# A two-layer sequence kernel, first chunk of layer 2: step sizes deferred, norm steps split over two engines, B rows copied from SBUF, filler matmuls in TensorE's gaps

## The chip, the cores and the metric

The kernel runs on one core of a Trainium2 chip, in float32 throughout. The metric is the device time of one launch in microseconds: 20159.46, the median of three runs (20150.19 to 20165.52).

## What is computed

The input is 16 images of 192 channels by 56 x 56, seen as 3136 tokens. Two residual layers follow each other, each behind a group norm without parameters:

```
x = x + L0(gn(x))     # RWKV: WKV recurrences forward and backward, gate, layer norm, output product
x = x + L1(gn(x))     # Mamba: below
# L1, for each token t:
x1 = layernorm(tok) ; x = x1 @ W_in_x.T ; z = x1' @ W_in_z.T
# once forward (f) and once backward (b) over the tokens:
xc  = silu(conv4(x) + conv_b)                  # depthwise, 4 taps, 384 channels
dbl = xc @ W_xproj.T                           # 12 columns for dt, 16 for B, 16 for C
dt  = softplus(dbl[:, :12] @ W_dt.T + dt_bias)
h   = h * exp(dt * A) + (dt * xc) * B          # 384 channels x 16 states, a scan over t
y   = sum over states of h * C + xc * D
out = ((y_f + y_b) * silu(z)) @ W_out.T + b_out
```

## The kernel before

A hardware loop runs over the 16 images; each turn is one block for layer 1 and one for layer 2, with all engines meeting in between (`build`, the loop at its end). Layer 2 is named `layer1_*` in the code, one function for each engine: `layer1_tensor`, `layer1_vector`, `layer1_scalar`, `layer1_pool` (GpSimd) and `layer1_sync` (SyncE, which issues all DMAs).

Layer 2 cuts the tokens into 7 chunks of T = 448 and walks them forward and then backward, 14 chunks (index `i`) in all. In a chunk there are EJ = 3 groups of 128 channels (`e` or `k`), and in a group NP = 8 pairs of states (`p`). The unit is a pair, numbered `q` over the whole layer: 24 in a chunk, 336 in all. For a pair, ScalarE makes two decays exp(dt A) in PSUM (`decay`, L1172) and the values at the pair's boundary (L1181, L1188); VectorE or GpSimd multiplies du = dt xc by two rows of B (`product`, L1021 on VectorE for pairs 1, 3, 4 and 6 of a group, L1232 on GpSimd for 0, 2, 5 and 7); VectorE scans (`scan`, L1032); GpSimd multiplies by two rows of C (`output`, L1240); TensorE sums the result over the states into PSUM by identity matmuls (L962).

What a chunk needs before its first pair is called side work. `side_schedule` puts each such step on its engine's list with a due time counted in pairs, and each engine runs, between its own pairs, what has come due (`Steps.due`, `side(g)`). Times below -10 are the entry of the layer, before any pair. The names of the steps: `ns` scales the input by the group norm (L1060), `n1` sums over channels (L893), `nc` subtracts the mean (L989, L991), `nq` squares (L1067), `n2` sums (L899), `nr` makes the inverse root (L1072, L1074), `nm` multiplies (L1215), `x` is the projection (L905), `xe` its way out of PSUM (L1086), `cv` the convolution by diagonal matrices (L919), `c1` to `c4` and `xc` the silu (L1094 to L1107, L996), `xp` the product for dt, B and C (L926), `p1` its copy to `res` in SBUF (L1114), `t` the product for the step size (L931), `t1` to `t3` and `td` the softplus (L1121 to L1130, L1001), `du` the product dt xc (L1221), `dp` its copy to PSUM for VectorE (L1134). `res` holds the 12 dt rows in partitions 0 to 11, B's 16 rows in partitions 32 to 47 and C's in 48 to 63.

A B or C row is needed in all 128 partitions. SyncE stores the 32 rows to DRAM (`cw`, L1286, 56 KB) and loads them back with every row repeated to 128 partitions, four rows at a time: `bl` (L1292) for B and `cl` (L1297) for C, k = 0 to 3, alternating, 896 KB each. Pair p needs `bl` number p // 2.

PSUM has eight banks: 0 to 3 hold the decays of two pairs, 4 holds du, 5 the sum y, 6 and 7 serve the side work. At the entry of the layer banks 0 to 3 serve side work as well, and the first decays wait until the side jobs in them are done. The entry does the whole chain for chunk 0 with all three groups' step sizes, in this order on the lists:

```
for e in range(EJ):
    step_size(i, e, t + u[e])
```

## Time and profile before

| | |
|---|---|
| median of 3 runs | 20159.46 us |
| profiled execution, its time | 20123.45 us |
| its span, first to last instruction | 20121.7 us |
| mean granted TensorE clock | 0.938 |
| TensorE matmuls, busy | 17468.9 us, 87% |
| VectorE, busy | 17219.6 us, 86% |
| GpSimd, busy | 16825.7 us, 84% |
| ScalarE, busy | 13992.6 us, 70% |
| DMA, mean share of 16 engines | 29.8% |

The profiled execution is one run of the same program. Times inside it count from the start of its span; the first image's layer 2 begins at 228.51. An L and a number is a line of the kernel before. A float32 matmul of the program appears as two instructions, each with its weight load.

### The profile page before, as it was taken

What the parts mean: (1) busy time and instruction counts of PE and PEld (TensorE: products, weight loads), DVE (VectorE), ACT (ScalarE), POOL (GpSimd) and SP (SyncE); (2) the same over time, 40 slices, a digit from 0 to 9 for tenths busy, and PEclk for the clock granted to TensorE, in tenths of its full rate; (3) what the DMA queues carried; (4) which work ended last, traced back from release to release, by engine and by line L of the source; (5) the groups of instructions that cost most, each with busy time, mean ns of one, the idle gap of its engine ahead of it and who ended that gap; (6) DMA issues with size and microseconds to landing.
All of it is one profiled execution on the core that took longest, in us unless ns stands there. A gap on an engine that the chain in (4) does not pass through costs nothing. (4 is left out here: it accounts for less than half of the span.)

```text
span 20121.7 us, 179901 instructions
## 1 busy us (share of the span) xinstructions
PE 17468.9 (87%) x43392; PEld 7664.0 (38%) x43392; DVE 17219.6 (86%) x13583; ACT 13992.6 (70%) x35077; POOL 16825.7 (84%) x10932
## 2 busy tenths in 40 slices
PE   7888988889888898888988889888898888988889
PEld 3433434334343343433434334343343433434334
DVE  7988979889798897988979789797897978979789
ACT  6767767577676776767767577675776767767677
POOL 6978969789697896978969799696996979969699
PEclk9989989899899998989989899898998989989899
DMA  2313323133231332313323133231332313323233
GB/s 85 135 65 129 137 76 134 65 129 137 76 134 66 128 137 76 134 65 128 137 77 133 66 128 136 77 133 65 129 136 76 134 65 135 130 77 135 73 132 124
DMA packets 528855, 2178.88 MB, mean 108 GB/s; under 512 B 96328, under 2 KB 243424, under 8 KB 527648
## 3 DMA queue, kind: packets, MB, share of 16 engines
q1 hardware_dynamic: 527648, 2165.99, 29.8%
q8 instruction: 366, 6.00, 0.1%
q14 instruction: 841, 6.89, 0.1%
HBM read 1905.47 MB, written 245.63 MB: 107 GB/s over the span
## 5 line engine op out<-in xcount | busy, mean ns | idle before, releaser
L1032 DVE TENSOR_TENSOR_SCAN arena<-ps,arena 128x897 f32<-128x897 f32 x5376 | 10963.7, 2066 | 993.9 <-ACT arena L1188 761.6
L1240 POOL TENSOR_TENSOR arena<-arena 128x896 f32<-128x896 f32 x5376 | 9427.4, 1769 | 901.5 <-PE ps L962 619.8
L962 PE MATMUL ps<-arena,ident 128*128 128x448 f32 x21504 | 8979.4, 556 | 879.6 <-POOL arena L1240 876.2
L1172 ACT ACTIVATE ps<-arena,A 128x448 f32<-128x448 f32 x10752 | 6412.1, 632 | 1749.0 <-DVE arena L1032 1705.3
L962 PEld LDWEIGHTS ps<-arena,ident 128*128 128x128 f32 x21504 | 4049.3, 193 | 5473.3 <-issue 3690.3
L1232 POOL TENSOR_TENSOR arena<-arena 128x896 f32<-128x896 f32 x2688 | 4773.6, 1776 | 0.2 <-DMA arena<-bc_rows 0.2
L1021 DVE TENSOR_TENSOR arena<-ps,arena 128x896 f32<-128x896 f32 x2688 | 2868.0, 1067 | 30.4 <-ACT ps L1134 30.4
L919 PE MATMUL ps<-arena,diag 128*128 128x448 f32 x5376 | 2178.4, 549 | 154.0 <-issue 141.8
L919 PEld LDWEIGHTS ps<-arena,diag 128*128 128x128 f32 x5376 | 1014.8, 192 | 1233.9 <-issue 1097.4
L1094 ACT ACTIVATE arena<-ps,vece 128x448 f32<-128x448 f32 x672 | 423.3, 630 | 948.5 <-PE ps L919 948.5
L1188 ACT ACTIVATE arena<-arena 128x2 f32<-128x2 f32 x5376 | 1045.8, 195 | 50.9 <-DVE arena L1032 50.9
L956 PE MATMUL ps<-arena,skipd 128*128 128x448 f32 x1344 | 720.3, 619 | 389.6 <-DVE arena L1008 268.0
L1221 POOL TENSOR_TENSOR arena<-arena 128x448 f32<-128x448 f32 x672 | 653.3, 980 | 461.7 <-DVE arena L1001 461.7
L774 POOL TENSOR_TENSOR arena<-arena 128x448 f32<-128x448 f32 x336 | 343.6, 1023 | 735.0 <-DVE arena L547 735.0
L1181 ACT ACTIVATE arena<-arena 128x1 f32<-128x1 f32 x4608 | 888.4, 193 | 0.0
L996 DVE TENSOR_TENSOR arena<-arena,ps 128x448 f32<-128x448 f32 x672 | 407.8, 607 | 436.7 <-ACT ps L1107 435.9
L593 PE MATMUL ps<-x,arena 96*128 96x448 f32 x1344 | 688.6, 651 | 77.1 <-DVE arena L563 46.9
L1215 POOL TENSOR_TENSOR arena<-arena 96x448 f32<-96x448 f32 x224 | 214.7, 979 | 628.6 <-ACT arena L1074 628.6
L905 PE MATMUL ps<-arena,wx 96*128 96x448 f32 x1344 | 601.7, 590 | 136.0 <-POOL arena L1215 136.0
L931 PE MATMUL ps<-arena,wdt 12*128 12x448 f32 x1344 | 665.3, 592 | 47.5 <-DVE arena L1001 37.4
L785 POOL TENSOR_TENSOR arena<-arena 128x448 f32<-128x448 f32 x336 | 359.9, 1071 | 404.2 <-ACT arena L731 404.2
L576 DVE TENSOR_TENSOR_SCAN ps<-ps,arena 128x898 f32<-128x898 f32 x336 | 680.4, 2025 | 3.1
(160 smaller groups left out, 19406.9 us busy)
## 6 DMA issues: line engine op xcount, KB each, us to landing
arena<-bc_rows SPq DMA_DIRECT2D x1792, 896.0 KB, 5.4
x_projected<-arena SPq DMA_DIRECT2D x112, 672.0 KB, 3.5
y_forward<-arena SPq DMA_DIRECT2D x112, 672.0 KB, 3.9
arena<-x_projected SPq DMA_DIRECT2D x112, 672.0 KB, 7.7
arena<-y_forward SPq DMA_DIRECT2D x112, 672.0 KB, 4.1
x<-in_x SPq DMA_DIRECT2D x119, 336.0 KB, 3.6
x_normed<-arena SPq DMA_DIRECT2D x112, 336.0 KB, 2.8
arena<-x_normed SPq DMA_DIRECT2D x112, 336.0 KB, 4.2
```

Source lines behind the costliest of these rows:

```text
L576: e.tensor_tensor_scan(atile(u), atile(u), bq[:, u % 3, :], 0.0, ALU.mult, ALU.add).then_inc(b_sc, 1)
L593: k = e.matmul(ps[:, b, 0:T], ws[:, i, o:o + 128], f[:, i, :], **last)
L919: m = e.matmul(o, diag[:, k, q, :], xh[i % 2][:, k, h:h + T], start=q == 0, stop=q == 3)
L956: e.matmul(y, skipd[:, s, k, :], xc[:, r % NXC, :], start=True, stop=False)
L962: m = e.matmul(y, ident[:, :], pr[:, q % NPR, a * T:a * T + T], start=False, stop=p == NP - 1 and a == 1)
L1021: e.tensor_tensor(two(bb[:, q % NB, :]), ps[:, DUBANK, 0:T].unsqueeze(1).to_broadcast([128, 2, T]), br[:, 2 * p:2 * p + 2, :], ALU.mult).t ...
L1032: e.tensor_tensor_scan(rev(hh[:, q % NH, 0:W2], s), rev(decays(q)[:, 0:W2], s), rev(bb[:, q % NB, 0:W2], s), car[:, k, n:n + 1] if i % NC ...
L1172: e.activation(two(decays(q))[:, a, :], dt[:, r % NDT, :], ACT.Exp, scale=Am[s][:, k, 2 * p + a:2 * p + a + 1]).then_inc(c_ex, 1)
L1181: e.activation(bb[:, q % NB, T:T1], car[:, k, n:n + 1] if i % NC else zero[:, 0, 0:1], ACT.Copy).then_inc(c_rs, 1)
L1188: e.activation(car[:, k, 2 * p:2 * p + 2], h[:, 0:T1 + 1:T1] if s else h[:, T - 1:W2:T1], ACT.Copy).then_inc(c_ca, 1)
L1232: e.tensor_tensor(two(bb[:, q % NB, :]), du[:, r % NDU, :].unsqueeze(1).to_broadcast([128, 2, T]), br[:, 2 * p:2 * p + 2, :], ALU.mult).th ...
L1240: e.tensor_tensor(pr[:, q % NPR, :].rearrange("p (a b) -> p a b", a=2), two(hh[:, q % NH, :]), cr[:, 2 * p:2 * p + 2, :], ALU.mult).then_i ...
```

## The change

Four things change, all at the entry of layer 2 in every image.

1. *Step sizes.* Of chunk 0, group 0's step size stays in the entry; those of groups 1 and 2 get the due times -1.9 and 1, so `t`, `t1` to `t3`, `td` and `du` of these run between the first pairs. Banks 0 to 3 serve only jobs below -10.
2. *Norm steps of chunk 0 on two engines.* `ns`, `nq` and `nm` do the first half (96 x 448) on ScalarE, ScalarE and GpSimd as before and the second half on VectorE.
3. *B's first four rows.* In chunk 0, SyncE copies rows 0 and 1 from `res` in SBUF to 128 partitions each (one DMA for a row, source one partition repeated 128 times, semaphore `s_bf`), then stores the 32 rows as before, then copies rows 2 and 3 in the same way; `bl` number 0 is left out. Pair 0 waits for `s_bf`, pair 1 for both copies of `s_bl[0]`.
4. *Fillers.* `busy(e, n, b)` issues n matmuls of constants, 128 x 384, into a bank that nobody reads then: five at the end of layer 1, two behind the statistics, two behind `n1`, three behind `n2`, three behind the last `cv`, one behind `xp`.

```diff
@@ -79,11 +79,12 @@
         act.append((max(NP * (EJ * i + e) - 2, t + 4.5), "dp", i, e))
 
     def project(i, t, u, v):
+
         pe.append((t, "xp", i, 0))
         act.append((t + v, "p1", i, 0))
         sp.append((t + 1.5, "cw", i, 0))
         for e in range(EJ):
-            step_size(i, e, t + u[e])
+            step_size(i, e, t + u[e] if i or not e else (-1.9, 1)[e - 1])
         for G in range(4):
             r = PER * i - NP + 2 * G
             sp.append((max(r + 1, t + 2), "bl", i, G))
@@ -103,6 +104,8 @@
             pe += [(t - 0.2, "n1", i, 0), (t + 2.1, "n2", i, 0)]
             act += [(t + 1.9, "nq", i, 0), (t + 3.0, "nr", i, 0), (t + 4.6, "xh", i, 0)]
             pool += [(t + 3.4, "nm", i, 0)]
+            if not i:
+                dve += [(t + 1.9, "nq", i, 0), (t + 3.4, "nm", i, 0)]
             sp += [(t + 5, "nw", i, 0), (t + 8, "xw", i, 0)]
             for e, (u, v) in enumerate(((4.2, 6.4), (4.3, 7.4), (6.2, 11))):
                 pe.append((t + u, "x", i, e))
@@ -136,11 +139,11 @@
     plans = [sorted(p, key=lambda a: a[0]) for p in (pe, act, dve, pool, sp)]
     jobs, used = {}, {}
     for k, (t, name, i, e) in enumerate(plans[0]):
-        banks = WBANK if t >= 0 else [*WBANK, 0, 1, 2, 3]
+        banks = WBANK if t >= -10 else [*WBANK, 0, 1, 2, 3]
         b = banks[k % len(banks)]
         jobs[name, i, e] = (k, b, used.get(b, 0))
         used[b] = used.get(b, 0) + 1
-        if t < 0:
+        if t < -10:
             first = dict(used)
     return plans, jobs, first
@@ -578,6 +581,11 @@
         w.wait_ge(b_ag, 2 + 2 * NC)
         for j in range(CJ):
             e.bn_aggr(mv[:, j, :], st[:, j, :, :].rearrange("p a b -> p (a b)"))
+
+    def busy(e, n, b):
+
+        for _ in range(n):
+            e.matmul(ps[:, b, 0:3 * 128], ident[:, :], skipd[:, 0, :, :].rearrange("p a b -> p (a b)"), start=True, stop=True)
 
     def layer0_tensor(e):
         w = Waits(e)
@@ -678,6 +686,8 @@
                 w.wait_ge(b_bv, U)
                 product(VB, 1, *divmod(U, 3)).then_inc(b_v, 1)
             side(U)
+        w.wait_ge(b_xo, nth(4, 1) + 1)
+        busy(e, 5, 3)
 
     def layer0_scalar(e):
         e.preload_act_table_set("natural_log_exp_and_others")
@@ -833,9 +843,10 @@
                                                             "taps_loaded", "x_stored"))
     s_xl, s_nl, s_yl = ([sem(f"{k}{b}") for b in range(2)] for k in ("xp_loaded", "n_loaded", "y_loaded"))
     s_bl, s_cl = ([sem(f"{k}{G}") for G in range(4)] for k in ("b_loaded", "c_loaded"))
+    s_bf = sem("b_first")
     sems1 = [n1.v, n1.t, n1.a, c_ex, c_rs, c_bv, c_bp, c_sc, c_ca, c_mc, c_sm, c_ya, c_yv, c_wt, *c_wf, c_ns, c_nc,
              c_nq, c_nr, c_nm, c_pad, c_xh, c_c1, c_c2, c_c3, c_c4, c_t1, c_t2, c_t3, c_du,
-             c_dp, c_z1, c_z2, c_z3, c_z4, c_g, s_nw, s_xw, s_yw, s_cw, s_dg, s_out, *s_xl, *s_nl, *s_yl, *s_bl, *s_cl]
+             c_dp, c_z1, c_z2, c_z3, c_z4, c_g, s_nw, s_xw, s_yw, s_cw, s_dg, s_out, *s_xl, *s_nl, *s_yl, *s_bl, *s_cl, s_bf]
 
     def filled(w, name, i, e=0):
         w.wait_ge(c_wt, jobs[name, i, e][0] + 1)
@@ -861,6 +872,13 @@
         b = DECAY[q % 2]
         return ps[:, b:b + 2, :].rearrange("p a b -> p (a b)")[:, 0:2 * T1]
 
+    def b_loaded(w, i, p):
+
+        if not i and not p:
+            w.wait_ge(s_bf, 32)
+        else:
+            w.wait_ge(s_bl[p // 2], 16 * (i + 1 + (p < 2)))
+
     def product_done(w, q):
 
         if ON_VECTOR[q // NP % EJ][q % NP]:
@@ -876,7 +894,11 @@
     def layer1_tensor(e):
         w = Waits(e)
         n1.tensor(e, w, 0)
+        busy(e, 2, DUBANK)
         steps = Steps(plan_pe)
+
+
+        behind = {("n1", 0): 2, ("n2", 0): 3, ("cv", 2): 3, ("xp", 0): 1}
 
         def job(name, i, k):
             _, b, n = jobs[name, i, k]
@@ -943,6 +965,8 @@
                         m = e.matmul(o[0:CP, :], wout[:, j, k * CP:(k + 1) * CP], gy[:, j, :],
                                      start=j == 0, stop=j == EJ - 1)
                     m.then_inc(c_wt, 1)
+                if not i:
+                    busy(e, behind.get((name, k), 0), DUBANK)
 
         side(-10)
         for g in range(-2, Q + LAG):
@@ -968,6 +992,8 @@
     def layer1_vector(e):
         w = Waits(e)
         w.wait_ge(n1.v, n1.vector(e, w, 0))
+        e.tensor_scalar(nrm[:, 0, T:2 * T], x1[:, 1, ch(0)], gs[:, 4, 1:2], gs[:, 5, 1:2], ALU.mult,
+                        ALU.add).then_inc(c_ns, 1)
         e.memset(xh[0][:, :, 0:3], 0.0).then_inc(c_pad, 1)
         for b in DECAY:
             e.memset(ps[:, b, T:T1], 0.0)
@@ -989,6 +1015,14 @@
                     e.tensor_tensor(o, o, ps[0:CP, b, 0:T], ALU.subtract).then_inc(c_nc, 1)
                     o = nrm[:, i % 2, T:2 * T]
                     e.tensor_tensor(o, o, ps[0:CP, b, 0:T], ALU.subtract).then_inc(c_wf[b], 1)
+                if name == "nq":
+                    freed(w, "n1", i)
+                    o = nrm[:, i % 2, T:2 * T]
+                    e.tensor_tensor(tmp[:, 1, :], o, o, ALU.mult).then_inc(c_nq, 1)
+                if name == "nm":
+                    w.wait_ge(c_nr, i + 1)
+                    o = nrm[:, i % 2, T:2 * T]
+                    e.tensor_tensor(o, o, tmp[:, 2, :], ALU.mult).then_inc(c_nm, 1)
                 if name == "xc":
                     w.wait_ge(c_c4, r + 1)
                     b = bank_of("cv", i, k)
@@ -1016,7 +1050,7 @@
         def product(q):
             r, i, k, p, s = pair(q)
             w.wait_ge(c_dp, r + 1)
-            w.wait_ge(s_bl[p // 2], 16 * (i + 1))
+            b_loaded(w, i, p)
             w.wait_ge(c_sc, q - NB + 1)
             e.tensor_tensor(two(bb[:, q % NB, :]), ps[:, DUBANK, 0:T].unsqueeze(1).to_broadcast([128, 2, T]),
                             br[:, 2 * p:2 * p + 2, :], ALU.mult).then_inc(c_bv, 1)
@@ -1056,14 +1090,14 @@
                     if i > 1:
                         filled(w, "x", i - 2, EJ - 1)
                         w.wait_ge(s_nw, 16 * (i - 1))
-                    for j in range(CJ):
+                    for j in range(CJ if i else 1):
                         e.activation(nrm[:, i % 2, j * T:j * T + T], x1[:, j, ch(c)], ACT.Identity,
                                      scale=gs[:, 4, j:j + 1], bias=gs[:, 5, j:j + 1]).then_inc(c_ns, 1)
                 if name == "nq":
                     freed(w, "n1", i)
                     w.wait_ge(c_nc, i + 1)
                     w.wait_ge(c_nm, 2 * i)
-                    for j in range(CJ):
+                    for j in range(CJ if i else 1):
                         e.activation(tmp[:, j, :], nrm[:, i % 2, j * T:j * T + T], ACT.Square).then_inc(c_nq, 1)
                 if name == "nr":
                     filled(w, "n2", i)
@@ -1210,7 +1244,7 @@
                 if name == "nm":
                     w.wait_ge(c_nr, i + 1)
                     freed(w, "n1", i)
-                    for j in range(CJ):
+                    for j in range(CJ if i else 1):
                         o = nrm[:, i % 2, j * T:j * T + T]
                         e.tensor_tensor(o, o, tmp[:, 2, :], ALU.mult).then_inc(c_nm, 1)
                 if name == "du":
@@ -1227,7 +1261,7 @@
         def product(q):
             r, i, k, p, s = pair(q)
             w.wait_ge(c_du, r + 1)
-            w.wait_ge(s_bl[p // 2], 16 * (i + 1))
+            b_loaded(w, i, p)
             w.wait_ge(c_sc, q - NB + 1)
             e.tensor_tensor(two(bb[:, q % NB, :]), du[:, r % NDU, :].unsqueeze(1).to_broadcast([128, 2, T]),
                             br[:, 2 * p:2 * p + 2, :], ALU.mult).then_inc(c_bp, 1)
@@ -1281,10 +1315,14 @@
             if name == "cw":
                 freed(w, "xp", i)
                 for G in range(4 if i >= 2 else 0):
-                    w.wait_ge(s_bl[G], 16 * (i - 1))
+                    w.wait_ge(s_bl[G], 16 * (i - (G > 0)))
                     w.wait_ge(s_cl[G], 16 * (i - 1))
+                for n in range(0 if i else 2):
+                    e.dma_start(br[:, n, :], res[32 + n:33 + n, :].unsqueeze(1).to_broadcast([1, 128, T])).then_inc(s_bf, 16)
                 e.dma_start(cd[i % 2], res[32:64, :]).then_inc(s_cw, 16)
-            if name == "bl":
+                for n in range(2, 2 if i else 4):
+                    e.dma_start(br[:, n, :], res[32 + n:33 + n, :].unsqueeze(1).to_broadcast([1, 128, T])).then_inc(s_bl[0], 16)
+            if name == "bl" and (i or k):
                 w.wait_ge(s_cw, 16 * (i + 1))
                 if i:
                     for q in (PER * i - NP + 2 * k, PER * i - NP + 2 * k + 1):
```

On SyncE, at chunk 0's store and loads (`bc_rows` is the DRAM tensor, `arena` is SBUF, `c_free0` the semaphore of `p1`), before:

```order
L1286 DMA bc_rows<-arena 32x448 [waits c_free0]
L1292 DMA arena<-bc_rows 128x1792 [waits bc_stored]
L1297 DMA arena<-bc_rows 128x1792
L1292 DMA arena<-bc_rows 128x1792
L1297 DMA arena<-bc_rows 128x1792
```

and with the change:

```order
L1321 DMA arena<-arena 128x1x448 [waits c_free0]
L1321 DMA arena<-arena 128x1x448
L1322 DMA bc_rows<-arena 32x448
L1324 DMA arena<-arena 128x1x448 x2
L1335 DMA arena<-bc_rows 128x1792 [waits bc_stored]
L1330 DMA arena<-bc_rows 128x1792
L1335 DMA arena<-bc_rows 128x1792
```

Four copies from `arena` to `arena` stand around the store, and the first load is now C's, where B's stood.

On GpSimd, from the norm's multiply on (96x448; then du, 128x448; B products, 128x2x448; output products, 128x896), before:

```order
L1215 TENSOR_TENSOR arena<-arena 96x448 [waits c_free6,c_nrs]
L1215 TENSOR_TENSOR arena<-arena 96x448
L1221 TENSOR_TENSOR arena<-arena 128x448 [waits c_free3,c_free1]
L1221 TENSOR_TENSOR arena<-arena 128x448 [waits c_free6,c_free2]
L1221 TENSOR_TENSOR arena<-arena 128x448 [waits c_free7,c_free3]
L1232 TENSOR_TENSOR arena<-arena 128x2x448 [waits b_loaded0,c_du]
L1232 TENSOR_TENSOR arena<-arena 128x2x448 [waits b_loaded1]
L1240 TENSOR_TENSOR arena<-arena 128x896 [waits c_loaded0,c_scan]
L1240 TENSOR_TENSOR arena<-arena 128x896 [waits c_scan]
L1240 TENSOR_TENSOR arena<-arena 128x896 [waits c_loaded1,c_scan]
L1232 TENSOR_TENSOR arena<-arena 128x2x448 [waits b_loaded2]
```

and with the change:

```order
L1249 TENSOR_TENSOR arena<-arena 96x448 [waits c_free6,c_nrs]
L1255 TENSOR_TENSOR arena<-arena 128x448 [waits c_free3,c_free1]
L1266 TENSOR_TENSOR arena<-arena 128x2x448 [waits b_first,c_du]
L1266 TENSOR_TENSOR arena<-arena 128x2x448 [waits b_loaded1]
L1274 TENSOR_TENSOR arena<-arena 128x896 [waits c_loaded0,c_scan]
L1274 TENSOR_TENSOR arena<-arena 128x896 [waits c_scan]
L1255 TENSOR_TENSOR arena<-arena 128x448 [waits c_free6]
L1274 TENSOR_TENSOR arena<-arena 128x896 [waits c_loaded1,c_scan]
L1266 TENSOR_TENSOR arena<-arena 128x2x448 [waits b_loaded2]
L1249 TENSOR_TENSOR arena<-arena 96x448 [waits c_free7,c_nrs]
L1249 TENSOR_TENSOR arena<-arena 96x448
```

The second and third du moved behind output products 2 and 4, and one half of the first multiply is gone; the second B product still stands ahead of the first output product.

On TensorE, from the statistics to the convolution, before:

```order
L333 MATMUL ps<-mv,grp 96x2
L335 MATMUL ps<-gs,grp 96x2 [waits c_stat_vec]
L893 MATMUL ps<-arena,ones 96x448 [waits c_nsc]
L893 MATMUL ps<-arena,ones 96x448
L899 MATMUL ps<-arena,ones 96x448 [waits c_nsq]
L899 MATMUL ps<-arena,ones 96x448
L905 MATMUL ps<-arena,wx 128x448 [waits c_nrm]
L905 MATMUL ps<-arena,wx 128x448 x5
L919 MATMUL ps<-arena,diag 128x448 [waits c_pad,c_free0]
```

and with the change:

```order
L336 MATMUL ps<-mv,grp 96x2
L338 MATMUL ps<-gs,grp 96x2 [waits c_stat_vec]
L588 MATMUL ps<-skipd,ident 128x384 x2
L915 MATMUL ps<-arena,ones 96x448 [waits c_nsc]
L915 MATMUL ps<-arena,ones 96x448
L588 MATMUL ps<-skipd,ident 128x384 x2
L921 MATMUL ps<-arena,ones 96x448 [waits c_nsq]
L921 MATMUL ps<-arena,ones 96x448
L588 MATMUL ps<-skipd,ident 128x384 x3
L927 MATMUL ps<-arena,wx 128x448 [waits c_nrm]
L927 MATMUL ps<-arena,wx 128x448 x5
L941 MATMUL ps<-arena,diag 128x448 [waits c_pad,c_free0]
```

L588 is the filler; the waits of the rows that were there are the same.

## Rows read from the trace of the kernel before

**Rows 1.** The page: busy us, share of the span and instructions of each engine.

```profile
PE 17468.9 (87%) x43392; PEld 7664.0 (38%) x43392; DVE 17219.6 (86%) x13583; ACT 13992.6 (70%) x35077; POOL 16825.7 (84%) x10932
```

**Rows 2.** Timeline of image 1: start us, us, engine, line, operation [idle before <-releaser].

```profile
223.66 1.00 PE L657 MATMUL ps<-arena,wo 64*96 64x448 f32 x4
...
230.99 1.41 ACT L1060 ACTIVATE arena<-x,gs 96x448 f32<-96x448 f32 x2 [0.22 <-DVE gs L328]
...
232.46 3.30 PE L893 MATMUL ps<-arena,ones 96*96 96x448 f32 x4 [2.35 <-ACT arena L1060]
...
236.98 1.04 ACT L1067 ACTIVATE arena<-arena 96x448 f32<-96x448 f32 x2 [4.57 <-DVE arena L991]
...
238.07 3.30 PE L899 MATMUL ps<-arena,ones 96*96 96x448 f32 x4 [2.31 <-ACT arena L1067]
...
242.73 1.91 POOL L1215 TENSOR_TENSOR arena<-arena 96x448 f32<-96x448 f32 x2 [38.97 <-ACT arena L1074]
```

**Rows 3.** The same timeline, from the projection x to p1.

```profile
244.69 7.66 PE L905 MATMUL ps<-arena,wx 96*128 96x448 f32 x12 [3.32 <-POOL arena L1215]
...
252.19 9.19 PE L919 MATMUL ps<-arena,diag 128*128 128x448 f32 x24
...
266.27 0.54 ACT L1114 ACTIVATE arena<-ps 64x448 f32<-64x448 f32 x1 [1.71 <-PE ps L926]
```

**Rows 4.** The same timeline, from the first step size on.

```profile
268.06 0.64 ACT L1121 ACTIVATE arena<-ps,vece 128x448 f32<-128x448 f32 x1 [1.25 <-PE ps L931]
...
275.33 0.98 POOL L1221 TENSOR_TENSOR arena<-arena 128x448 f32<-128x448 f32 x1 [0.69 <-DVE arena L1001]
...
276.26 3.50 POOL L1232 TENSOR_TENSOR arena<-arena 128x896 f32<-128x896 f32 x2
...
278.16 3.93 DVE L1032 TENSOR_TENSOR_SCAN arena<-ps,arena 128x897 f32<-128x897 f32 x2
...
280.25 1.76 POOL L1240 TENSOR_TENSOR arena<-arena 128x896 f32<-128x896 f32 x1 [0.49 <-DVE arena L1032]
...
285.38 1.67 PE L899 MATMUL ps<-arena,ones 96*96 96x448 f32 x4
```

**Rows 5.** GpSimd's groups, 280 to 349 us: busy, mean ns, idle before.

```profile
L1240 POOL TENSOR_TENSOR arena<-arena 128x896 f32<-128x896 f32 x24 | 42.1, 1766 | 6.4 <-DVE arena L1032 4.9 <-PE ps L962 1.5
```

**Rows 6.** Windows: us, five engines busy, PEclk granted, DMA share, GB/s.

```profile
222.00:226.00 4.00, 2.66 (x10) 0.81 (x8) 3.86 (x8) 0.00 (x0) 0.00 (x0) 1.00 0.00 0
...
232.50:235.70 3.20, 3.20 (x4) 0.91 (x4) 0.00 (x0) 0.00 (x0) 0.00 (x0) 0.50 0.00 0
```

**Rows 7.** VectorE's groups, 194 to 230 us.

```profile
L516 DVE TENSOR_TENSOR arena<-arena 128x448 f32<-128x448 f32 x2 | 1.4, 698 | 0.0
```

**Rows 8.** DMA issues (KB, us to landing); then the first and third load alone.

```profile
arena<-arena SPq DMA_DIRECT2D x128, 112.0 KB, 2.2
bc_rows<-arena SPq DMA_DIRECT2D x224, 56.0 KB, 1.6
```

```profile
L1292 SPq DMA_DIRECT2D arena<-bc_rows x1: 343/343/343, 268.4 to 268.4; - x1
...
DMA to landing us min/median/max: 4.5/4.5/4.5
```

```profile
L1292 SPq DMA_DIRECT2D arena<-bc_rows x1: 432/432/432, 269.3 to 269.3; - x1
...
DMA to landing us min/median/max: 8.3/8.3/8.3
```

**Rows 9.** Windows while DMAs read 128, 64 and 32 partitions of SBUF.

```profile
255.00:255.50 0.50, 0.50 (x2) 0.21 (x2) 0.00 (x0) 0.10 (x1) 0.00 (x0) 1.00 1.02 383
87.10:87.60 0.50, 0.00 (x0) 0.00 (x0) 0.50 (x2) 0.50 (x2) 0.50 (x1) 1.00 0.89 204
267.65:267.85 0.20, 0.20 (x2) 0.03 (x1) 0.00 (x0) 0.00 (x0) 0.00 (x0) 0.50 0.99 224
```

## The prediction

> **What bounds the kernel now.** I read the page's busy shares first [rows 1]. No engine is idle much: TensorE 87%, VectorE 86%, GpSimd 84%. The change touches only the stretch in which each image enters layer 2, so the page's averages say little about it. I therefore read the timeline from the end of layer 1 (image 1, 223 to 282 us), then the landing times of the DMAs there, then windows with the granted clock and the DMA rate. One image stands for all 16: each of them shows this stretch once.
>
> The entry is a chain in which one engine works at a time. From 230.99 on, ScalarE scales both halves of the input, TensorE sums, VectorE subtracts, ScalarE squares, TensorE sums again, ScalarE takes the inverse root, GpSimd multiplies [rows 2]. Then come the projection x, the convolutions, the product xp and the copy p1, which ends at 266.81 [rows 3]. I call that moment P. After P, three groups' step sizes are computed before GpSimd's first B product at 276.26 and the first scan at 278.16, P+11.35 [rows 4]. From there on GpSimd is nearly full: over the first chunk its output products alone take 42.1 us and wait 6.4 us [rows 5].
>
> TensorE runs much of this entry at the lower of its two levels, 1.2 of 2.4 GHz: the granted clock is 1.00 from 222 to 226 and 0.50 from 232.5 to 235.7 [rows 6]. The same four instructions of 448 columns take 3.30 us there [rows 2] and 1.67 us in chunk 1's norm at 285.38 [rows 4]. In between the engine had no dense work from 224.66 to 232.46.
>
> **Up to P, part by part.**
> - *Fillers.* Nothing reads them. The five at layer 1's end start at 224.66, behind the last L657 [rows 2]. Each is two instructions of 384 columns; at 1.67/4 = 0.42 per 448 columns at most, ten cost 3.6 us and end by 228.3, inside the wait for the next block at 228.51. Those behind n1 (1.4 us) fit the 2.3 us before n2, those behind n2 (2.1 us) the 3.3 before x, those behind the last convolution (2.1 us) the 3.9 between the last convolution's end (261.38) and the last third of xp, of which the first two thirds need 1.5. The one behind xp costs t at most 0.1. Hence zero, if the clock stays up; at half clock they double, and the cover over n1 and n2 is overrun by about 2 us together.
> - *What the clock gives.* n1 and n2 go from 3.30 to 1.67: 2 x 1.63. The 12 instructions of x start at 244.69 and hand over at 252.19 [rows 3]; at the upper level 12 x 0.375 = 4.5, so 3.0 less. The 24 of the convolutions take 9.19, 0.38 each, and gain nothing. Sum 6.3. The bounds are 6.3 and, with the fillers useless, minus 2. I take 6.3, since the work up to 226 ran at 1.00 and the fillers leave no gap near today's eight microseconds.
> - *Norm steps on two engines.* The scaling takes 1.41 on ScalarE alone; halved, 0.70 less. The squares take 1.04; VectorE's nearest row, L516, takes 0.70 [rows 7], so 0.3 less. The multiply takes 1.91 on GpSimd; GpSimd's half is 0.98, so 0.9 less if both run together. Sum 1.9; the bounds are 1.2 (the multiply's halves in turn, 0.98 + 0.70) and 1.9. I take 1.9: two products of GpSimd take 3.50 from 276.26 although VectorE's first scan starts beside them [rows 4].
> - The Trainium skill (SBUF — State Buffer, "Who interferes with whom") says a VectorE instruction with two SBUF inputs and a GpSimd instruction that reads SBUF exclude each other. By that rule the multiply would gain 0.2 instead of 0.9, 11 us over 16 images; no row of this entry shows the pair.
>
> P comes 6.3 + 1.9 = 8.2 us earlier.
>
> **After P.** The later groups' step sizes leave the path. What remains: t's product (1.2 us from P to L1121), four passes of ScalarE of 0.54 to 0.64 (2.3), at most 0.70 on VectorE, 0.98 for du, 1.75 for the product [rows 3, 4]: with the hand-overs scan 0 could start at about P+7.3, 4 us earlier, **if B is there**. The two du move in behind scans 0 and 1: 2 x 0.98 on GpSimd, which is the full engine; the td go to VectorE, the t1 to t3 to ScalarE.
>
> **B's first rows decide.** Now: the store lands 1.6 us after its issue, and the first load (bl0), issued at 268.43, lands 4.5 later, at P+6.1. The third (bl1) lands at 277.6, P+10.8, just before GpSimd's second product at about P+11.2 [rows 8]. So loads land 2.3 us apart.
>
> The change sends each of four rows 128 times out of one partition: 128 x 1792 B = 229 KB per row, 0.92 MB in all, as much as the load it replaces. No row shows a DMA with one source partition. The nearest ones [rows 9]: a store out of 128 partitions, 383 GB/s at a share of 1.02; a copy from 64 partitions to 64, 204 GB/s at 0.89; the store out of 32 partitions, 224 GB/s at 0.99. A busy DMA engine thus moves 23.5 GB/s in the first case and 14.2 in the other two: with fewer partitions two engines share a path of about 28 GB/s, they don't each keep theirs. If all 16 queue at the one path of partition 32 (33, 34, 35), a row takes 229/28 = 8.1 us. Ends of the range: 0.6 us per row (no shared path, 383 GB/s) and 9.8 us (one engine's 23.5). I take 8.1, which is what the nearest rows say of a path.
>
> The Trainium skill (SBUF — State Buffer, "Door 1: The DMA port swizzle") puts partitions 32 to 35 on one port and gives 27.6 GB/s measured over four partitions; that would be 8.3 us a row and 0.8 us more per image than my sum. It speaks against this part of the change.
>
> Then rows 0 and 1 land at about P + 1.6 + 16.2 = P+17.9 (1.6 is the small copy's 2.2 without its 0.6 of transfer). The store's packets stand behind them and rows 2 and 3 behind those; all four are through by P+34. The load cl0, issued when the store lands, has its packets behind rows 2 and 3 and lands at P+36.2, bl1 at P+38.4 (2.3 each). On GpSimd the second product (pair 2, needs bl1) stands ahead of the first output product. So it starts at P+38.4, the output product at P+40.2 instead of P+13.4: 26.8 later. Add 2.0 for the two du, subtract 4 of the 6.4 us that GpSimd idled in this chunk: 24.8. Against 8.2 earlier: 16.6 us later per image, 266 us in 16. The profiled execution's 20123 becomes 20389; the median of the runs lies 36 above it, so **20425 us**. With 7 to 9.8 us a row, and with the clock's share uncertain, this case spans 20320 to 20545.
>
> **Rivals.**
> - *The rows leave at full rate (28%).* Each row takes 0.6 us, rows 0 and 1 land by P+3.5, and the store by P+3.2 to 3.7. Then bl1 becomes what the first chunk waits for: issued at about P+3.7, it lands at P+10.0, GpSimd's second product ends at P+11.8 and the output product starts 1.6 earlier than now. The du fit into the 6.4 us of idle. 8.2 + 1.8 = 10 us per image, 160 in all: 20000. For it: the load out of DRAM repeats its source 128 times too, at full rate (0.92 MB per 2.3 us). Against it: the lower rate per engine in [rows 9].
> - *A path twice as wide (9%).* At 4 us a row all four are through by P+17, bl1 lands at P+21.6, the output product starts 10 later; with du and idle 8 remains against 8.2: within 0.2% of now, 20160.
> - *The fillers don't hold the clock.* Then 8.2 shrinks to about 0 (minus 2 of the fillers, plus 1.9); it shifts either case by up to +130 us. It decides nothing about the sign in the first case, and is in the ranges.
> - *The loads don't matter because the step sizes bound the start.* Scan 0 waits today for td and du, not for B; but B has only 3 us of slack there (276.26 against 272.9), and 16 us of transfer don't fit in.
>
> **Numbers.** Shared path 63%, full rate 28%, wider path 9%. A measurement of this kernel tells 0.2% (40 us) from no change. Faster: 0.29 (the full rate, a little of the middle). Same: 0.08. Slower: 0.63. The range must reach into both cases: 19980 to 20540; the likeliest case's own is 20320 to 20545.
>
> **What would show it.** Right: the four single-row copies out of SBUF land 16 us and more after issue; GpSimd's and VectorE's first products wait for DMAs; the DMA rate in that stretch is near 28 GB/s; the first output product starts some 40 us after p1; PEclk is 1.00 from the block's start to P, n1 and n2 at 1.67, P at 30 us after the block's start instead of 38.3. Wrong: landings of 2 to 4 us for these copies, a first scan near P+7.3, and GpSimd's second product waiting for bl1 at P+10.

## The result, and the profile after

The changed kernel takes **20450.1 us** (median of 4 runs, 20445.8 to 20463.2); the kernel before took 20154.8 us beside it (4 runs, 20132.9 to 20165.5). The ratio of the two sets of runs is **1.0151, 95% interval 1.0136 to 1.0166**: 1.5% slower. (The quotient of the two medians is 1.0147; ratios below, too, can differ from the quotient of the medians by some 0.0005.) The forecast was 20425 us, in the case of the shared path. The profiled execution took 20451.14 us (span 20449.3), so here it lies at the median; the profiled execution of before, 20123.45, lay 36 below the median of its first three runs.

The timeline of image 1 after the change, in the stretch that the prediction is about (start us, us, engine, line, operation [idle before <-releaser]). The block of layer 2 opens with ScalarE's table load at 231.47.

```profile
227.55 3.49 PE L588 MATMUL ps<-skipd,ident 128*128 128x384 f32 x10
...
231.47 1.28 ACT L1079 ACT_TABLE_LOAD   x1 [14.40 <-PEq L1356]
...
234.47 1.74 PE L915 MATMUL ps<-arena,ones 96*96 96x448 f32 x4 [0.30 <-ACT arena L1094]
...
241.17 0.62 DVE L1025 TENSOR_TENSOR arena<-arena 96x448 f32<-96x448 f32 x1 [3.11 <-ACT arena L1108]
241.21 1.41 POOL L1249 TENSOR_TENSOR arena<-arena 96x448 f32<-96x448 f32 x1 [34.49 <-ACT arena L1108]
...
242.68 4.78 PE L927 MATMUL ps<-arena,wx 96*128 96x448 f32 x12 [0.89 <-POOL arena L1249]
...
261.38 0.54 ACT L1148 ACTIVATE arena<-ps 64x448 f32<-64x448 f32 x1 [1.71 <-PE ps L948]
```

These are the rows that answer to [rows 2, 3]. The four instructions of n1 take 1.74 instead of 3.30, x takes 4.78 instead of 7.66, and p1 ends at 261.92: P, the end of the copy p1, is 30.45 behind the table load, where it was 38.3 in image 1 of before. The ten instructions of the five fillers at layer 1's end are done at 231.04, 0.43 before the table load.

Behind P, the same timeline:

```profile
261.94 1.18 SPq L1321 DMA_DIRECT2D arena<-arena  x2
...
263.15 5.64 SPq L1322 DMA_DIRECT2D bc_rows<-arena  x1
...
268.84 10.55 SPq L1324 DMA_DIRECT2D arena<-arena  x2
...
281.44 1.77 POOL L1266 TENSOR_TENSOR arena<-arena 128x896 f32<-128x896 f32 x1 [14.31 <-DMA arena<-arena]
282.42 4.62 SPq L1335 DMA_DIRECT2D arena<-bc_rows  x1
287.08 8.54 SPq L1330 DMA_DIRECT2D arena<-bc_rows  x1
...
298.16 1.09 DVE L1055 TENSOR_TENSOR arena<-ps,arena 128x896 f32<-128x896 f32 x1 [32.09 <-DMA arena<-arena]
...
303.03 1.77 POOL L1266 TENSOR_TENSOR arena<-arena 128x896 f32<-128x896 f32 x1 [19.82 <-DMA arena<-bc_rows]
304.76 3.48 POOL L1274 TENSOR_TENSOR arena<-arena 128x896 f32<-128x896 f32 x2
```

They answer to [rows 4]. GpSimd's first B product waits 14.31 us for a copy, VectorE's 32.09 us, and GpSimd's next one 19.82 us for the load bl1. The first output product starts at 304.76, P+42.8, where it was P+13.4. On the page the waits are these:

```profile
L1266 POOL TENSOR_TENSOR arena<-arena 128x896 f32<-128x896 f32 x2688 | 4768.3, 1774 | 543.9 <-DMA arena<-bc_rows 315.3
L1055 DVE TENSOR_TENSOR arena<-ps,arena 128x896 f32<-128x896 f32 x2688 | 2862.1, 1065 | 513.5 <-DMA arena<-arena 513.5
```

Before, the same two groups had waited 0.2 and 30.4 us. The copies' landing times, rows 0 and 1 and then rows 2 and 3 (views of the lines L1321 and L1324; the three durations in ns are those of the issue on SyncE, the landing times count from the start of the issue):

```profile
L1321 SPq DMA_DIRECT2D arena<-arena x32: 524/563/596, 261.9 to 19398.0; - x32
...
DMA to landing us min/median/max: 10.7/14.8/18.8
```

```profile
L1324 SPq DMA_DIRECT2D arena<-arena x32: 1958/5256/8547, 268.8 to 19412.9; - x32
...
DMA to landing us min/median/max: 20.6/21.4/22.1
```

And windows of the same kernel (us, five engines, granted clock, DMA share, GB/s): the statistics, n1 of chunk 0, n1 of chunk 1, and the copies:

```profile
231.50:234.00 2.50, 1.86 (x8) 1.07 (x8) 1.12 (x6) 2.01 (x4) 0.00 (x0) 1.00 0.03 7
234.50:236.20 1.70, 1.70 (x5) 0.88 (x6) 0.00 (x0) 0.00 (x0) 0.00 (x0) 1.00 0.00 0
269.30:272.50 3.20, 3.20 (x4) 0.90 (x4) 0.00 (x0) 3.10 (x7) 0.00 (x0) 0.50 0.90 27
264.00:280.00 16.00, 3.30 (x4) 0.96 (x4) 0.62 (x1) 7.64 (x16) 0.98 (x1) 0.61 0.89 27
```

The granted clock of TensorE, which was 0.50 in the norm (1.2 of 2.4 GHz) [rows 6], is 1.00 through chunk 0's norm now. During the copies the 16 DMA engines are busy nine tenths of the time and move 27 GB/s together; in [rows 9] shares of 0.89 to 1.02 went with 204 to 383. In this kernel a high DMA share alone says little of how much moves.

One image is no mean, so for this kernel and all that follow I read four marks from the trace in each of the 16 images: the table load that opens the block, P, the starts of the first scan and the first output product (counted from P), and the start of the 25th scan, the first of chunk 1. The last column is the ratio of the times to before, with its interval, where there is one. Each kernel is compared with runs of before taken beside it: e1 to e4 with 15 runs (median 20140.2), e5 to e8 with 15 (20115.3), e9 to e12 with 9 (20130.6).

| kernel | block to P | first scan | first output | 25th scan | ratio |
|---|---|---|---|---|---|
| before | 38.60 | 11.13 | 13.23 | 81.16 | 1 |
| the change | 30.44 | 37.26 | 42.70 | 111.13 | 1.0151 (1.0136 to 1.0166) |
| e1: without the SBUF rows | 30.44 | 7.95 | 12.47 | 81.12 | 0.9922 (0.9909 to 0.9936) |
| e2: the SBUF rows alone | 38.68 | 37.26 | 42.75 | 109.94 | 1.0217 (1.0201 to 1.0232) |
| e3: fillers alone | 32.00 | 10.90 | 13.00 | 80.92 | 0.9919 (0.9905 to 0.9932) |
| e4: deferred step sizes alone | 38.59 | 7.91 | 12.43 | 81.14 | 0.9997 (0.9988 to 1.0006) |
| e5: norm split alone | 36.00 | 12.03 | 14.13 | 82.16 | 1.0002 (0.9993 to 1.0011) |
| e6: e1, bl1 ahead of cl0 | 30.44 | 7.96 | 10.83 | 81.16 | 0.9929 (0.9915 to 0.9942) |
| e7: e1, fillers after P too | 30.44 | 7.98 | 12.49 | 79.77 | 0.9915 (0.9901 to 0.9928) |
| e8: rows from partitions 32 to 47 | 30.44 | 12.72 | 18.91 | 87.10 | one run |
| e9: rows from 16 of partitions 0 to 60 | 30.44 | 7.88 | 13.88 | 81.24 | one run |
| e10: two SBUF rows | 30.44 | 24.44 | 29.92 | 97.94 | 1.0052 (1.0037 to 1.0067) |
| e11: e7 and e6 together | 30.44 | 7.97 | 10.88 | 79.70 | 0.9915 (0.9901 to 0.9928) |
| e12: e3 less the five at layer 1's end | 33.02 | 10.89 | 12.99 | 80.91 | 0.9953 (0.9939 to 0.9966) |

### The profile page after: what moved, and what is told of

Same layout as the page of the kernel before. It is cut to its first block and busy times, and to the rows that moved or that the text cites. A ratio compares the mean times of both kernels' runs of the same rounds, so it can differ in the third digit from the quotient of the medians.

```text
span 20449.3 us, 181005 instructions
## 1 busy us (share of the span) xinstructions
PE 17559.7 (86%) x43904; PEld 7728.2 (38%) x43904; DVE 17248.8 (84%) x13631; ACT 13972.7 (68%) x35045; POOL 16791.7 (82%) x10916
## 5 line engine op out<-in xcount | busy, mean ns | idle before, releaser
L1128 ACT ACTIVATE arena<-ps,vece 128x448 f32<-128x448 f32 x672 | 423.2, 630 | 954.5 <-PE ps L941 954.5
L1215 ACT ACTIVATE arena<-arena 128x1 f32<-128x1 f32 x4608 | 886.4, 192 | 0.0
L1155 ACT ACTIVATE arena<-ps,vece 128x448 f32<-128x448 f32 x672 | 422.7, 629 | 362.8 <-PE ps L953 362.8
L700 ACT ACTIVATE arena<-ps 128x448 f32<-128x448 f32 x336 | 182.1, 542 | 670.6 <-PE ps L606 226.6
```

The costliest lines, as they stand in the source:

```text
L1215: e.activation(bb[:, q % NB, T:T1], car[:, k, n:n + 1] if i % NC else zero[:, 0, 0:1], ACT.Copy).then_inc(c_rs, 1)
```

## The experiments

### e1: all of the change but the SBUF rows

```diff
-        if not i and not p:
-            w.wait_ge(s_bf, 32)
-        else:
-            w.wait_ge(s_bl[p // 2], 16 * (i + 1 + (p < 2)))
+        w.wait_ge(s_bl[p // 2], 16 * (i + 1))
...
-                for n in range(0 if i else 2):
-                    e.dma_start(br[:, n, :], res[32 + n:33 + n, :].unsqueeze(1).to_broadcast([1, 128, T])).then_inc(s_bf, 16)
...
-            if name == "bl" and (i or k):
+            if name == "bl":
```

> The change without its third part: B's first four rows come from DRAM again, all else stays. Theory (the one-partition copies cost all of the loss): the first scan no longer waits for copies; P (end of p1) stays about 30.5 us after the block's start, the first output product starts about 1.6 us earlier after P than before (13.4), so about 10 us per image less than the kernel before: ratio to before near 0.992 (0.990 to 0.995). Rival (the deferred step sizes on the full GpSimd, or the fillers, cost as well): ratio 0.996 to 1.002.

19974.9 us (5 runs, 19959.5 to 19989.4) against 20140.2 (15 runs), 165 us less. Without the copies the rest of the change gains 0.8%, and the first scan starts at P+7.95; the prediction had P+7.3 "if B is there". So the loss is the copies' alone, as expected. The first output product comes 0.8 us earlier than before, not the 1.6 expected, since it waits for the load bl1 (see e6).

### e2: the SBUF rows alone, on the kernel before

The diff is the change's part 3 on before: `b_loaded`, the four copies and the left-out load.

> The third part alone on the kernel before. Theory: the first output product starts about 43 us after P as in the changed kernel, against 13.4 before, so 28 to 30 us per image more: ratio 1.022 to 1.024. Rival (the copies are slow only because the deferral and the idle hand-over put other work beside them): ratio under 1.015.

20570.3 us (4 runs, 20565.4 to 20579.5), 430 us more than before, 26.9 per image, a ratio just under the 1.022 to 1.024 expected. The marks behind P are those of the changed kernel within 0.1 us up to the first output; the 25th scan is 1.2 us earlier. In this kernel no du stand behind the scans, which would account for it. With both parts taken apart, 0.9922 and 1.0217 make 1.0137, near the 1.0151 measured.

### e3: the fillers alone, on the kernel before

```diff
+        w.wait_ge(b_xo, nth(4, 1) + 1)
+        busy(e, 5, 3)
...
+        busy(e, 2, DUBANK)
+        behind = {("n1", 0): 2, ("n2", 0): 3, ("cv", 2): 3, ("xp", 0): 1}
```

Besides these lines it has the helper `busy` and its call behind each job of chunk 0, as in the change.

> The fillers alone on the kernel before. Theory: the granted clock is 1.00 from the block's start to P, n1, n2 and x run at 1.67 to 1.75 and 4.5 us, P comes about 6 us earlier, and as nothing behind P depends on it: 6 us per image, ratio 0.995. But B's loads move with P too, so nothing is lost there. Rival (ScalarE and the loads bound the entry): ratio 0.998 to 1.000.

19978.5 us (5 runs, 19959.2 to 19980.9), 162 us less: as much as e1 gained with three parts, and more than the 0.995 expected. P comes 6.60 us earlier (6.3 had been forecast for the clock), n1, n2 and x take 1.74, 1.75 and 4.78 us as in the changed kernel. 6.6 in 16 images is 106 us; some 56 us more lie elsewhere in the image (see e12).

### e4: the deferred step sizes alone

```diff
-            step_size(i, e, t + u[e])
+            step_size(i, e, t + u[e] if i or not e else (-1.9, 1)[e - 1])
```

With it goes the change's new limit of -10 for banks 0 to 3.

> The deferred step sizes alone on the kernel before. Theory: the first scan comes 3 to 4 us earlier after P, but the second product waits for the third load (P+10.8), and GpSimd has two du more in the chunk: 1 to 2 us per image gained, ratio 0.998 to 0.999. Rival (the du on the full GpSimd cost more than the earlier start brings): ratio 1.000 to 1.002.

20132.7 us (11 runs), ratio 0.9997: nothing that can be measured, where 1 to 2 us per image had been expected. Yet the first scan starts 3.2 us earlier. GpSimd's timeline of image 1 shows where the 3.2 us go:

```profile
283.78 3.48 POOL L1240 TENSOR_TENSOR arena<-arena 128x896 f32<-128x896 f32 x2
287.22 0.98 POOL L1221 TENSOR_TENSOR arena<-arena 128x448 f32<-128x448 f32 x1
288.16 1.76 POOL L1240 TENSOR_TENSOR arena<-arena 128x896 f32<-128x896 f32 x1
289.88 1.77 POOL L1232 TENSOR_TENSOR arena<-arena 128x896 f32<-128x896 f32 x1
294.98 1.91 POOL L1215 TENSOR_TENSOR arena<-arena 96x448 f32<-96x448 f32 x2 [3.32 <-ACT arena L1074]
296.85 1.76 POOL L1240 TENSOR_TENSOR arena<-arena 128x896 f32<-128x896 f32 x1
```

Chunk 1's norm multiply (L1215) stands in GpSimd's order behind three output products and waits 3.32 us for ScalarE's inverse root (2.3 in the mean of the images). In the kernel before it waits for nothing (289.60, behind L1232). The head start runs into chunk 1's norm chain; the fourth output starts at P+24.4 in both kernels in the mean of the images (the last row above is a late one, P+25.6), and from the 12th scan on the two agree within 0.1 us.

### e5: the norm split alone

```diff
+        e.tensor_scalar(nrm[:, 0, T:2 * T], x1[:, 1, ch(0)], gs[:, 4, 1:2], gs[:, 5, 1:2], ALU.mult,
+                        ALU.add).then_inc(c_ns, 1)
...
-                    for j in range(CJ):
+                    for j in range(CJ if i else 1):
```

The squares `nq` and the multiply `nm` are split in the same way; it is the whole of the change's part 2.

> The norm steps on two engines, alone on the kernel before. By the prediction's terms 1.9 us per image less up to P (1.2 if the halves of the multiply exclude each other): ratio 0.9985 to 0.999. Rival (the window in which the granted clock comes back does not move with the work, so the projection only runs longer at the lower level): P - 0 to 0.5 us, ratio 1.000.

20116.7 us (11 runs) against 20115.3 (15 runs): no difference. In the trace P comes 2.6 us earlier, more than the 1.9 of the norm steps, since the projection x also takes less (6.94 for 7.66 in image 1). 0.9 of it is lost again before the first scan. The first four instructions of t now take 0.84 us each, at a granted clock of 0.50 from their start; the kernel before needed 1.91 for its first three, at 0.82 over the first 1.1 us:

```profile
268.51 3.35 PE L933 MATMUL ps<-arena,wdt 12*128 12x448 f32 x4 [0.63 <-ACT arena L1126]
```

At the 25th scan 1.6 us remain, 26 us in all. The interval reaches down to 14 us gained; the one profiled execution (20071.4) is also the lowest of the 11. What became of the rest isn't settled. Alone, the fillers and the split give 6.60 and 2.60 up to P, together 8.16, so they share 1.0 us; x's 0.7 is the larger part of it.

### e6: e1 with the load bl1 ahead of cl0

```diff
-            sp.append((max(r + 3, t + 2.1), "cl", i, G))
+            sp.append((max(r + (3 if i else 3.5), t + 2.1), "cl", i, G))
```

> e1 (B from DRAM) with the second B load ahead of the first C load, in the first chunk. It lands about 8.5 us after P instead of 10.8. Theory A (the wait for this load takes back what the deferral gives): the first output product 1.8 us earlier and the 25th scan too, ratio to before 0.9905 to 0.991. Theory B (the chunk is held at P+22.7 by GpSimd's multiply for chunk 1's norm, whose chain runs on TensorE at the lower clock): the first output products come earlier, the 25th scan doesn't; ratio 0.992 as e1.

19969.9 us (5 runs), ratio 0.9929, as e1. In e1 GpSimd's second B product waits for bl1:

```profile
273.17 1.77 POOL L1263 TENSOR_TENSOR arena<-arena 128x896 f32<-128x896 f32 x1 [2.89 <-DMA arena<-bc_rows]
```

Here the first output comes 1.6 us earlier, and the fourth one at P+24.5 as in e1. Rival 1 of the prediction named this load as the next bound. It is next in order, but chunk 1's norm multiply starts at P+22.6 here as in e1, e4 and before (means of the images), so what the load gives isn't seen.

### e7: e1 with fillers behind the first t and chunk 1's norm sums

```diff
-        behind = {("n1", 0): 2, ("n2", 0): 3, ("cv", 2): 3, ("xp", 0): 1}
+        behind = {("n1", 0, 0): (2, DUBANK), ("n2", 0, 0): (3, DUBANK), ("cv", 0, 2): (3, DUBANK),
+                  ("xp", 0, 0): (1, DUBANK), ("t", 0, 1): (7, YBANK), ("n1", 1, 0): (5, YBANK)}
```

> e1 with fillers also in the two TensorE gaps behind P: seven behind the second group's step product, five behind chunk 1's n1, in the bank of y. Theory B (the first chunk is held by chunk 1's norm chain at the lower clock): n1, the last step product, the skip product and the first sums take half, GpSimd's multiply for chunk 1 starts 2 to 4 us earlier than P+22.7, and the 25th scan with it: ratio 0.989 to 0.991. Theory A (the load bl1 holds it): 0.992 as e1. If the later convolutions of chunk 1 pin it anyway, 0.992 too, with the multiply earlier.

The chain that seems to hold e4 and e6 runs at the lower level: in the changed kernel chunk 1's first norm sums are 3.30 us at a granted clock of 0.50 (window 269.30:272.50 above). With fillers around it, the timeline of e7 reads:

```profile
274.70 1.74 PE L913 MATMUL ps<-arena,ones 96*96 96x448 f32 x4 [0.66 <-ACT arena L1091]
...
276.29 3.39 PE L588 MATMUL ps<-skipd,ident 128*128 128x384 f32 x10
...
280.77 1.01 PE L951 MATMUL ps<-arena,wdt 12*128 12x448 f32 x2 [1.09 <-DVE arena L1032]
```

The norm multiply of chunk 1 on GpSimd waits for ScalarE's inverse root, in image 1 of e1 and then of e7:

```profile
285.01 1.92 POOL L1246 TENSOR_TENSOR arena<-arena 96x448 f32<-96x448 f32 x2 [2.24 <-ACT arena L1105]
```

```profile
288.16 1.92 POOL L1246 TENSOR_TENSOR arena<-arena 96x448 f32<-96x448 f32 x2 [0.44 <-ACT arena L1105]
```

In the mean of the images it moves from P+22.55 to P+21.20, the fourth output from P+24.4 to P+23.1 and the 25th scan by 1.35 us: the head start is held by this chain, shown by shortening it. The gain is less than the 2 to 4 us expected. The fillers quickened more than the norm's own sums. The products that stand ahead of the second sums in TensorE's order, the last of t, the skip product and the first sums over the states, went from 1.86, 1.86 and 2.84 us (image 1 of e1) to 1.01, 1.02 and 1.67 (image 1 of e7). Which of them counts wasn't separated. The time is 19949.7 us (5 runs, 19927.4 to 19958.1). 1.35 in 16 images is 22 us, less than the intervals tell, so that e7 beats e1 rests on the trace alone. It beats both kernels clear of the noise.

### e8: the copies read sixteen neighbouring partitions

```diff
-                    e.dma_start(br[:, n, :], res[32 + n:33 + n, :].unsqueeze(1).to_broadcast([1, 128, T])).then_inc(s_bf, 16)
+                    e.dma_start(br[:, n, :], res[32:48, :].unsqueeze(1).to_broadcast([16, 8, T])).then_inc(s_bf, 16)
```

The same for rows 2 and 3.

> The changed kernel with each of the four one-row copies reading 16 neighbouring partitions (32 to 47) eight times each instead of one partition 128 times; same bytes, same number of packets; B's first four rows are then mixed rows. Theory (four neighbouring partitions share a path of 28 GB/s): 229 KB over 4 paths, 2.0 us a row, the four copies through by about P+10, the first output product near P+21, time 20100 to 20200. Rival (each partition has a path of its own): 0.6 us a row as from 128 partitions, landings of 2.2 to 3.5 us, time near 19990. Rival (the source does not matter, it is the number of small packets): 8 us a row as before, time near 20450.

One run, 20056.3 us, a little under the 20100 to 20200 expected. Bytes and packets are those of the changed kernel, only the sources differ; so the number of small packets isn't what made the copies slow. The views of the first copies and of a window beside them:

```profile
L1321 SPq DMA_DIRECT2D arena<-arena x32: 592/598/627, 263.6 to 19030.4; - x32
...
DMA to landing us min/median/max: 4.4/5.3/6.3
```

```profile
268.00:270.00 2.00, 0.00 (x0) 0.00 (x0) 0.00 (x0) 2.00 (x5) 0.76 (x1) 0.50 0.92 106
```

106 GB/s is four times the 27 of one partition, not sixteen times. So four sources share what one has; with e9, where sources four apart get more, these are four neighbours.

### e9: the copies read sixteen spread partitions

```diff
-                    e.dma_start(br[:, n, :], res[32 + n:33 + n, :].unsqueeze(1).to_broadcast([1, 128, T])).then_inc(s_bf, 16)
+                    e.dma_start(br[:, n, :], res[0:64:4, :].unsqueeze(1).to_broadcast([16, 8, T])).then_inc(s_bf, 16)
```

The same for rows 2 and 3.

> The changed kernel, but each of the four one-row copies reads sixteen partitions spread over the whole of 0 to 60, every fourth one, instead of one partition for all 128 (so the B and C rows are mixed and the output is not the reference's; the bytes and the number of packets are the same). The run before this one read the neighbouring partitions 32 to 47 and moved 104 GB/s, four times the 27 GB/s of one partition. Theory A (only groups of four neighbours share a path): sixteen sources lie in sixteen groups, the sixteen DMA engines run at the full rate of some 200 to 380 GB/s, and the first copies land 2 to 4 us after issue. Theory B (a path is also shared by partitions 32 apart): eight paths of 26 GB/s, 208 GB/s, first copies in 3 to 4 us, all four within 5. Theory C (the source does not matter beyond four paths): landings as in the run before, 4.4 to 6.5 us. Time by A 19980 to 20020 us, by B 20000 to 20040, by C 20056.

```profile
L1321 SPq DMA_DIRECT2D arena<-arena x32: 564/582/594, 258.5 to 18940.3; - x32
...
DMA to landing us min/median/max: 3.0/3.3/3.6
```

```profile
260.00:262.00 2.00, 0.40 (x2) 0.00 (x0) 0.03 (x1) 1.88 (x4) 0.00 (x0) 1.00 1.01 198
```

198 GB/s at a full DMA share: Theory C falls. Sixteen groups of four would allow 16 x 27; the rate is that of eight, as Theory B had it (partitions 32 apart share), and as the copy from 64 partitions had shown (204, [rows 9]). A limit of some 200 GB/s on any copy inside SBUF would give the same rate, though; no run has such a copy with sources above partition 63, so that rival stays open. The time, 19963.9 us, is below what either theory gave and equal to e1's: even when the rows leave SBUF fast, part 3 gains nothing, because the first scan is at P+7.88 against 7.95 from DRAM, and behind it stands chunk 1's chain.

### e10: two rows by copies, two by a load

```diff
-                for n in range(2, 2 if i else 4):
-                    e.dma_start(br[:, n, :], res[32 + n:33 + n, :].unsqueeze(1).to_broadcast([1, 128, T])).then_inc(s_bl[0], 16)
...
+                a = 0 if i or k else 2
+                e.dma_start(br[:, 4 * k + a:4 * k + 4, :],
+                            cd[i % 2, 4 * k + a:4 * k + 4, :].unsqueeze(0).to_broadcast([128, 4 - a, T])).then_inc(s_bl[k], 16)
```

The semaphore waits are set to match.

> The changed kernel with two one-row copies instead of four: rows 2 and 3 of the first groups' B come from the scratch tensor in DRAM after the store, as all B rows did before. Theory A (one path of 27 GB/s, shared by whatever reads those partitions, and everything issued behind it waits): rows 0 and 1 still land at P+19.5, but the store is through by then, the loads behind it are no longer backed up, the first output product comes at about P+26 instead of P+42.8, so 13 to 14 us per image over the version without any copy: 20185 to 20200 us, a ratio of 1.002 to 1.005 to the kernel before; SyncE's issues behind the store return to under 1 us each, those ahead of it may stay long. Theory B (the loss is a fixed delay of the queue whatever is copied): the ratio stays at 1.012 or more. Theory C (two rows are hidden beside the chain of chunk 1's norm): under 0.998.

20238.8 us (4 runs, 20225.4 to 20250.3). Theory A holds in kind: half the rows, somewhat over half the loss (0.0130 of 0.0229 above e1's ratio), and SyncE's issues behind the store take 0.35 to 0.54 us again in the mean of the images. The time lies 39 us above the 20200 at which its range ended. Its P+26 was 3.9 us short: the store lands at P+19.1, only then the load goes out, and VectorE's product that waits for it starts 4.2 us later.

```profile
286.32 1.77 POOL L1266 TENSOR_TENSOR arena<-arena 128x896 f32<-128x896 f32 x1 [13.84 <-DMA arena<-arena]
286.38 0.34 SPq L1329 DMA_DIRECT2D arena<-bc_rows  x1
...
290.56 1.09 DVE L1055 TENSOR_TENSOR arena<-ps,arena 128x896 f32<-128x896 f32 x1 [19.13 <-DMA arena<-bc_rows]
```

The first output is at P+29.92, and the 25th scan 16.8 us later than in e1. The table now shows a pattern for this kernel: in e8, e10 and the change the 25th scan stands 68.0 to 68.4 us behind the first output. Up to P+13 or 14 a delay of the first output costs nothing (e6, e1 and e9: 10.83, 12.47 and 13.88, with the 25th scan at 81.2 each time); beyond that each us costs one.

### e11: the load's order, with the chain shortened

It is e7 with e6's line.

> The fastest version so far (the changed kernel without the on-chip copies, with fillers behind the first group's t and chunk 1's norm products) with the load bl1 issued ahead of cl0. The order alone brought the first output product 1.6 us earlier and nothing in the time when chunk 1's norm chain was cold. Theory A (the chunk is still held by chunk 1's norm and TensorE's products behind it): the ratio to the kernel before is that of the version with the old order, 0.9905 to 0.9920, and the eighth group's output does not move by over 0.3 us. Theory B (with the chain shortened the load is what is late): another 1 us per image, 19930 us, ratio 0.9905 or less.

19966.8 us (5 runs), 0.9915 like e7; the fourth output moves from P+23.1 to P+23.0. Theory A: the load still doesn't bound.

### e12: the fillers without the five at layer 1's end

```diff
-        w.wait_ge(b_xo, nth(4, 1) + 1)
-        busy(e, 5, 3)
```

> The kernel before with the fillers alone, less those at layer 1's end. With all fillers the block of layer 2 took 6.6 us less to P and the time was 0.9919 of the kernel before. Theory A (each filler holds the clock only for the products next to it): without those five the block's first norm products run at the lower level again, 3.3 instead of 1.7 us, and P comes 1.6 us later: ratio 0.9930 to 0.9937. Theory B (the clock, once fallen at layer 1's end, stays low through the products x as well): P comes 4 to 6 us later, ratio 0.996 to 0.998. Theory C (the five do nothing for this block): ratio 0.9919 within 0.0005.

20039.4 us (5 runs, 20016.0 to 20063.6), between theories A and B. The windows, from the two fillers behind the statistics to those behind n1:

```profile
229.70:232.20 2.50, 2.50 (x5) 1.16 (x5) 0.44 (x5) 1.82 (x4) 0.00 (x0) 0.50 0.00 0
232.40:234.30 1.90, 1.90 (x5) 0.83 (x5) 0.00 (x0) 0.00 (x0) 0.00 (x0) 0.80 0.04 9
234.30:235.70 1.40, 1.40 (x5) 0.57 (x3) 1.15 (x2) 0.02 (x1) 0.00 (x0) 1.00 0.00 0
```

The two fillers run at the lower level and overrun into n1; the clock rises within n1, and from there the block is as in e3. That costs 1.0 us up to P, 16 us in all; the time is 61 us more than e3's (0.0034 by the ratios), and the two intervals don't touch. So the five fillers give some 3 us per image elsewhere, the same us that e3 has beyond its 6.6. Between these two traces they split into 1.5 us in layer 1 and 1.3 us behind the 25th scan, and both stretches vary by several us from image to image, so no cause can be read from them. The length of layer 1 in these traces takes values from 188 to 200 us from image to image, mostly near 188, 192.5, 193.5 and 197, and its mean (194.3 before, 191.8 in e3, 193.3 here, but 193.1 in e1) doesn't tell it either. This stays open.

## Why the prediction was right

**Up to P: right, 8.16 us for 8.2.** The clock's part was 6.3 and is 6.60 (e3). The norm's was 1.9 and is 1.56 on top (32.00 to 30.44). Its mis-sized term is the multiply: VectorE's half and GpSimd's half start together at 241.17 and 241.21, but GpSimd's takes 1.41 instead of 0.98, so the pair ends after 1.45 instead of 1.91: 0.46 gained, not 0.9. The rule of the Trainium skill (SBUF — State Buffer, "Who interferes with whom") that the two exclude each other would have given 0.2 by the estimate in the prediction; the row lies between it and my 0.9, nearer to it. The trace agrees that GpSimd's half is held up, by 0.43 us, though not by the whole of VectorE's 0.62. The squares gave 0.4 for 0.3, the scaling 0.65 for 0.7.

**Fillers cost nothing: right within 0.15 us.** The groups ahead of n1, n2 and x end before TensorE's next operand is there. The one behind the last convolution holds the first two thirds of xp, as forecast, and these still end 0.31 us before the last third can start. The one behind xp costs t a little: its first instruction starts 0.20 us behind P, and 0.05 without fillers. The two overruns feared at half clock didn't come, except in e12, where they were built.

**The shared path: right, and what decides.** 8.1 us a row was forecast from 28 GB/s. Row 0 lands at P+10.8, row 3 at P+36.2 (means of the images): 8.5 us a row, 27 GB/s. The Trainium skill (SBUF — State Buffer, "Door 1: The DMA port swizzle") had 27.6 GB/s, from which the estimate was 8.3 us; the row agrees, and e8 agrees with its four partitions to a port. The fixed part was 1.6 and is 2.3. Hence rows 0 and 1 at P+19.4 for 17.9, rows 2 and 3 at P+36.2 for 34, bl1 at P+40.9 for 38.4, the first output at P+42.7 for 40.2.

**Du and idle: the term that failed most.** I added 2.0 for two du and took 4 off, since GpSimd idled 6.4 us in the chunk [rows 5]. The same view of the changed kernel, 304 to 375 us:

```profile
L1274 POOL TENSOR_TENSOR arena<-arena 128x896 f32<-128x896 f32 x24 | 42.1, 1767 | 2.6 <-DVE arena L1066 2.1 <-PE ps L986 0.6
...
L1255 POOL TENSOR_TENSOR arena<-arena 128x448 f32<-128x448 f32 x4 | 3.9, 978 | 0.0
L1249 POOL TENSOR_TENSOR arena<-arena 96x448 f32<-96x448 f32 x2 | 1.9, 975 | 1.9 <-ACT arena L1108 1.9
```

2.6 us of the idle time remain and 1.9 new ones stand before chunk 1's multiply: only 1.9 were absorbed, while the four du (3.9 instead of 2.0) came in full. From the first output to the 25th scan it is 68.4 us now and was 67.9; it is 67.2 in e2, where the du stand in front. So delay alone absorbs 0.7, and the du cost 1.2, if nothing else between these two kernels differs there.

**The sum.** 24.8 later behind P was forecast, 29.97 came: 2.7 from the first output, 2.5 from this term. Against 8.16, that is 21.8 per image at the 25th scan, where 16.6 was forecast. Of the 5.2 us, 1.7 are given back in the rest of the image: the profiled executions are 20.1 apart per image (1255.6 and 1275.7 from table load to table load). The runs' medians are 18.5 apart (295.3 in 16), since the execution of before was a low one. These two covered part of the mis-sized terms, and the median came to lie 25 us above the forecast. So close a hit is luck; that the shared path decides, and the sign with it, is what the runs show.

**The rivals.** Full rate did not come, but e9 made it come nearly so: 19964 us where that rival had 20000. Its next bound was misnamed (e6). "The loads don't matter" is right up to P+13 and wrong beyond it (e10).
